# An adaLN block with linear attention and a mixture of experts: new order of the work on every engine, and two f32 products made one split f32r product

## The reference, cut to what matters

```python
mod = (_silu(L0_c) @ L0_wmod).reshape(16, 6, 1, -1)
sa, ca, ga, sb, cb, gb = mod[:, 0], mod[:, 1], ...
ga, gb = sign(g) * max(|g|, 0.25)                      # both gates
h = _layernorm(x) * (1 + ca) + sa
# attention: 16 heads of 8 channels
q, k, v = h @ Wq.T + bq, h @ Wk.T + bk, h @ Wv.T + bv
q = softmax(q over the 8 channels of a head);  k = softmax(k over the tokens)
state = k^T v                                         # 8 x 8 for each head
out = q @ state
out = (out - mu) * rsqrt(var + eps) * ln_g + ln_b
x = x + ga * (out @ Wo.T + bo)
h = _layernorm(x) * (1 + cb) + sb
# experts: the router's softmax over 8, the best 2 of them by probability p
x = x + gb * sum over the two of p_e * (gelu(h @ w_in[e] + b_in[e]) @ w_out[e] + b_out[e])
```

## Time and profile before

| | |
|---|---|
| median of 3 runs | 392.75 us (391.49 to 393.89) |
| profiled execution, its own time | 392.8 us |
| its span (first to last instruction) | 391.1 us |
| TensorE busy | 362.9 us, 93% |
| VectorE busy | 282.5 us, 72% |
| ScalarE busy | 278.5 us, 71% |
| GpSimd busy | 216.8 us, 55% |

### The profile page before, as it was taken

The page is one execution under the profiler, slowest core; times in us unless marked ns, Lnnn a source line. Parts: engine busy times, 40 slices in busy tenths (PEclk is TensorE's granted clock), DMA queues, the critical chain, the costliest instruction groups (busy, mean ns, idle before and its releaser), DMA issues.

```text
span 391.1 us, 8091 instructions
## 1 busy us (share of the span) xinstructions
PE 362.9 (93%) x2502; PEld 327.3 (84%) x2502; DVE 282.5 (72%) x1060; ACT 278.5 (71%) x502; POOL 216.8 (55%) x221
## 2 busy tenths in 40 slices
PE   3657789999999999999999999999999999999995
PEld 3446679889999999899899999898998999988875
DVE  2665586787777888878877778788788787786432
ACT  3333679688787969696887879696969878675740
POOL 2315447373938466483838384664837383754543
PEclk9966579999999999999999999999999999999999
DMA  5570051240706071321606070605224150605061
GB/s 182 151 297 2 0 173 73 80 193 24 247 5 242 29 225 47 157 115 41 231 33 241 3 244 27 240 32 168 106 104 169 38 208 3 217 28 216 32 227 41
DMA packets 18817, 47.83 MB, mean 122 GB/s; under 512 B 2571, under 2 KB 6102, under 8 KB 18518
## 3 DMA queue, kind: packets, MB, share of 16 engines
q1 hardware_dynamic: 18576, 46.90, 33.3%
q10 hardware_dynamic: 198, 0.41, 0.3%
HBM read 42.82 MB, written 4.48 MB: 121 GB/s over the span
## 4 chain that ended last, share of the span: by engine, by line
PE 66%; DVE 9%; issue 6%; DMA 6%; POOL 5%; SPq 4%; ACT 2%; POOLq 0%; DVEq 0%; ACTq 0%
PE pY L684 19%; PE pH L672 6%; PE pH L674 6%; PE pH L673 6%; PE pB L661 4%; PE pQV L641 4%; PE pC L629 4%; PE pC L648 3%; POOL v L355 2%; DVE qn L876 2%; DMA gate_bc<-route_scratch 2%; DMA gates<-gate_scratch 2%; SPq L236 2%; DVE elg_cut L934 2%; PE pA L588 2%
## 5 line engine op out<-in xcount | busy, mean ns | idle before, releaser
L684 PE MATMUL pY<-wout,v 128*128 128x128 f32 x1024 | 128.7, 277 | 1.0 <-DVE v L958 0.7
L684 PEld LDWEIGHTS pY<-wout,v 128*128 128x128 f32 x1024 | 121.7, 193 | 2.2 <-DVE v L958 1.1
L502 ACT ACTIVATE u<-pH,cols 128x512 f32<-128x512 f32 x128 | 86.4, 689 | 49.5 <-PE pH L674 42.8
L344 POOL TENSOR_TENSOR rstd_o<-ve_o,neg_half 128x4 f32<-128x4 f32 x16 | 22.0, 1376 | 104.3 <-DVE ve_o L895 104.3
L958 DVE TENSOR_TENSOR v<-u,gate_bc 128x512 f32<-128x512 f32 x80 | 68.6, 860 | 7.0 <-DMA gate_bc<-route_scratch 3.7
L355 POOL TENSOR_TENSOR v<-u,gate_bc 128x512 f32<-128x512 f32 x48 | 63.7, 1329 | 9.0 <-DMA gate_bc<-route_scratch 9.0
L672 PE MATMUL pH<-h_hi,win_hi 128*128 128x512 f32 x128 | 54.9, 429 | 1.4 <-ACT u L502 1.4
L673 PE MATMUL pH<-h_hi,win_lo 128*128 128x512 f32 x128 | 50.6, 395 | 0.0
L674 PE MATMUL pH<-h_lo,win_hi 128*128 128x512 f32 x128 | 50.5, 394 | 0.0
L349 POOL TENSOR_TENSOR h_lo<-h,h_hi 128x512 fp32r<-128x512 f32 x16 | 22.5, 1405 | 20.2 <-ACT h_hi L440 20.2
L452 ACT ACTIVATE xn<-x_all,nmr,rstd 128x128 f32<-128x128 f32 x64 | 26.2, 482 | 4.5 <-POOL nmr L372 4.5
(11 more groups left out here) (151 smaller groups left out, 781.5 us busy)
## 6 DMA issues: line engine op xcount, KB each, us to landing
gate_bc<-route_scratch SPq DMA_DIRECT2D x64, 512.0 KB, 5.7
x_all<-in_L_attn_x SPq DMA_DIRECT2D x16, 256.0 KB, 6.9
out<-x_all SPq DMA_DIRECT2D x16, 256.0 KB, 2.0
gates<-gate_scratch SPq DMA_DIRECT2D x1, 2048.0 KB, 7.1
gb_bc<-gb_scratch SPq DMA_DIRECT2D x1, 1024.0 KB, 4.6
route_scratch<-gateT SPq DMA_DIRECT2D x64, 4.0 KB
win<-in_L_ffn_w_in SPq DMA_DIRECT2D x1, 512.0 KB, 5.6
wout<-in_L_ffn_w_out SPq DMA_DIRECT2D x1, 512.0 KB, 6.9
```

The costliest lines, as they stand in the source:

```text
L344: pool.tensor_tensor(rstd_o[:, :], ve_o[:, :], neg_half[:, :], ALU.pow).then_inc(s["rstdo_ready"], 1)
L502: act.activation(u[:, e % U, :], pH[:, e % 2, :], ACT.Gelu_apprx_tanh, bias=cols[:, e:e + 1]).then_inc(s["gelu_done"], 1)
L684: i = mm(pY[:, t * P:(t + 1) * P], v[:, e % U, t * P:(t + 1) * P], wout[:, e, :], start=False, stop=(e == NE - 1), skip_group_check=True)
```

## The change

The kernel after computes the same by the same tiles. Nine things differ.

1. `attend_centred` and `attend_project` are one function, `attend`: for each of the four token tiles three f32r products with both halves of the state weights at once (256 columns), q and the state weights each split in a high and a low part. `qT_evac` and `sw_evac` write the high parts, and two new DVE functions, `q_low` and `sw_low`, the low parts. The result goes to `pQV`, where qv of the next batch goes too, so `qv(n)` now waits for `residual1(n - 1)`.
2. Each engine's order is new: the start of it written out call by call, then a loop over a new `step(b)`, on TensorE with the last batches written out too.
3. TensorE runs ahead further: in step `b` the hidden products of `b + 1` stand beside qv and state of `b + 3` and hT and kT of `b + 4`.
4. On ScalarE the exp of the router stands between two gelus; the program has 53 table loads, 33 before.
5. In TensorE's start stand 30 calls of `keep_clock`, an f32 product of 256 columns whose result nobody reads.
6. The gates' and the gain's products come behind hT(0), and `expert_low`, `expert_bias` and the like between the first batches' functions.
7. x of a batch has one of four semaphores, and four loads can be under way.
8. The attention's gates are loaded in two transfers: of the first two batches, and of the others later. `spread_gates` is called once for each of a batch's four parts.
9. Wk and Wo are loaded by ScalarE's queue.

```diff
         def _(sp):
-            sp.dma_start(x_all[:, 0, :, :], x_v[0]).then_inc(s["x_loaded"], DMA)
-            for j, wt in enumerate((Wq, Wv, Wk, Wo)):
+            def load_x(n):
+                w(sp, f"x{n % XS}_loaded", DMA * (n // XS))
+                sp.dma_start(x_all[:, n, :, :], x_v[n]).then_inc(s[f"x{n % XS}_loaded"], DMA)
+
...
+            def spread_first_gates():
                 sp.wait_ge(s["gates_stored"], DMA)
-                sp.dma_start(gates[:, :, :, :].rearrange("p b w c -> p (b w c)"),
-                             gate_scratch.rearrange("(a b) n -> a (b n)", a=1).to_broadcast([P, NB * 2 * P])).then_inc(s["gates_loaded"], DMA)
-
-            def spread_moe_gates():
+                sp.dma_start(gates[:, 0:FIRST, :, :].rearrange("p b w c -> p (b w c)"),
+                             gate_scratch[0:FIRST, :].rearrange("(a b) n -> a (b n)", a=1).to_broadcast([P, FIRST * 2 * P])).then_inc(s["first_gates"], DMA)
+
+            def spread_later_gates():
+                sp.wait_ge(s["gates_stored"], DMA)
+                sp.dma_start(gates[:, FIRST:NB, :, :].rearrange("p b w c -> p (b w c)"),
+                             gate_scratch[FIRST:NB, :].rearrange("(a b) n -> a (b n)", a=1).to_broadcast([P, (NB - FIRST) * 2 * P])).then_inc(s["gates_loaded"], DMA)
+
+            def store_moe_gates():
                 sp.wait_ge(s["gb_ready"], 1)
                 sp.dma_start(gb_scratch, gb_rows[:, :]).then_inc(s["gb_stored"], DMA)
+
...
+                act.activation(qT_hi[:, :], pQT, ACT.Copy).then_inc(s["qT_ready"], 1)
 
             def sw_evac(n):
                 act.wait_ge(s["sw_done"], n + 1)
                 act.wait_ge(s["kinv_ready"], n + 1)
-                w(act, "cen_done", n)
-                w(act, "proj_done", n)
-                act.activation(sw[:, :, :].rearrange("p a c -> p (a c)"), pSW, ACT.Copy, scale=kinv[:, 0:1]).then_inc(s["sw_ready"], 1)
+                w(act, "att_done", n)
...
             def step(b):
+                if has(b + 2):
+                    exp_q(b + 2)
                 if has(b + 1):
-                    ln2_apply(b + 1)
+                    h2_evac(b + 1)
+                if has(b + 3):
+                    h_evac(b + 3)
+                if has(b):
+                    gelu(b, 4)
+                if has(b + 2):
+                    qT_evac(b + 2)
+                    sw_evac(b + 2)
+                if has(b + 1):
+                    exp_router(b + 1)
                 if has(b):
                     gelu(b, 5)
                 if has(b + 2):
-                    exp_k(b + 2)
-                if b == -1:
-                    expert_parts()
-                if has(b + 1):
-                    h2_evac(b + 1)
-                if has(b + 2):
-                    exp_q(b + 2)
-                    ek_evac(b + 2)
-                if has(b + 3):
-                    ln1_apply(b + 3)
-                if has(b + 1):
-                    exp_router(b + 1)
-                if has(b):
-                    gelu(b, 6)
-                if has(b + 2):
-                    sw_evac(b + 2)
-                    qT_evac(b + 2)
+                    out_square(b + 2)
                 if has(b + 1):
                     gateT_evac(b + 1)
                 if has(b):
+                    gelu(b, 6)
...
+            exp_k(0)
+            exp_q(0)
+            ek_evac(0)
+            expert_high()
...
+            def keep_clock():
+                pe.wait_ge(s["siluT_ready"], 1)
+                pe.wait_ge(s["wmod_loaded"], DMA)
+                mm(pH[:, 0, 0:2 * P], ident[:, :], wmod_sb[:, 0:2, :].rearrange("p a c -> p (a c)"), start=True, stop=True)
 
...
-            def attend_centred(n):
-                pe.wait_ge(s["sw_ready"], n + 1)
-                pe.wait_ge(s["qT_ready"], n + 1)
-                for t in range(T):
-                    i = mm(pQT[:, t * P:(t + 1) * P], qT[:, t * P:(t + 1) * P], sw[:, 1, :], start=True, stop=True)
-                i.then_inc(s["cen_done"], 1)
-
-            def attend_project(n):
-                pe.wait_ge(s["sw_ready"], n + 1)
-                pe.wait_ge(s["qT_ready"], n + 1)
-                for t in range(T):
-                    i = mm(pC[:, t * P:(t + 1) * P], qT[:, t * P:(t + 1) * P], sw[:, 0, :], start=True, stop=True)
-                i.then_inc(s["proj_done"], 1)
+            def attend(n):
+                pe.wait_ge(s["swlow_ready"], n + 1)
+                pe.wait_ge(s["qlow_ready"], n + 1)
+                for t in range(T):
+                    o = pQV[:, t, :, :].rearrange("p a c -> p (a c)")
+                    ts = slice(t * P, (t + 1) * P)
+                    mm(o, qT_hi[:, ts], sw_hi[:, :], start=True, stop=False)
+                    mm(o, qT_hi[:, ts], sw_lo[:, :], start=False, stop=False)
+                    i = mm(o, qT_lo[:, ts], sw_hi[:, :], start=False, stop=True)
+                i.then_inc(s["att_done"], 1)
 
...
+                hidden(b + 1, 0)
+                hidden(b + 1, 1)
+                combine(b, 4)
+                hidden(b + 1, 2)
+                hidden(b + 1, 3)
+                combine(b, 5)
+                qv(b + 3)
+                combine(b, 6)
+                combine(b, 7)
+                ek_back(b + 3)
+                hidden(b + 1, 4)
+                h2T(b + 2)
+                hidden(b + 1, 5)
+                hT(b + 4)
+                moe_bias(b + 1)
+                state(b + 3)
+                logits(b + 2)
+                q_turn(b + 3)
+                state_weights(b + 3)
+                combine(b + 1, 0)
+                combine(b + 1, 1)
+                hidden(b + 1, 6)
+                kT(b + 4)
+                attend(b + 3)
+                combine(b + 1, 2)
+                gate_turn(b + 2)
+                hidden(b + 1, 7)
+
+
+            turn_weights()
...
+            def q_low(n):
+                dve.wait_ge(s["qT_ready"], n + 1)
+                w(dve, "att_done", n)
+                dve.tensor_tensor(qT_lo[:, :], pQT, qT_hi[:, :].bitcast(F32), ALU.subtract).then_inc(s["qlow_ready"], 1)
+
+            def sw_low(n):
+                dve.wait_ge(s["sw_ready"], n + 1)
+                w(dve, "att_done", n)
+                dve.scalar_tensor_tensor(out=sw_lo[:, :], in0=pSW, scalar=kinv[:, 0:1], in1=sw_hi[:, :].bitcast(F32),
+                                         op0=ALU.mult, op1=ALU.subtract).then_inc(s["swlow_ready"], 1)
...
-                    state_out(b + 2)
-                    q_norm(b + 2)
-                    k_inv(b + 2)
+                    q_low(b + 2)
+                    sw_low(b + 2)
                 if has(b + 1):
                     gates_out(b + 1)
...
```

More of the change, by code:

```diff
@@ L545, in _ @@
+            exp_k(9)
+            ln2_apply(8)
+            ek_evac(9)
+            for b in range(7, 17):
                 step(b)
@@ new lines, in _ @@
+            kT(2)
+            keep_clock()
+            gate_turn(0)
+            keep_clock()
+            ek_back(2)
+            qv(2)
+            moe_bias(0)
+            hT(3)
+            keep_clock()
+            keep_clock()
+            hidden(0, 0)
+            hidden(0, 1)
+            state(2)
+            kT(3)
+            state_weights(2)
+            hidden(0, 2)
+            q_turn(2)
+            combine(0, 0)
+            hidden(0, 3)
+            hidden(0, 4)
+            h2T(1)
@@ new lines, in _ @@
+            hidden(0, 5)
+            attend(2)
+            hidden(0, 6)
+            combine(0, 1)
+            logits(1)
+            combine(0, 2)
+            hidden(0, 7)
+            qv(3)
+            ek_back(3)
+            combine(0, 3)
+            combine(0, 4)
+            combine(0, 5)
+            state(3)
+            hT(4)
+            hidden(1, 0)
+            gate_turn(1)
+            hidden(1, 1)
+            combine(0, 6)
+            combine(0, 7)
+            state_weights(3)
@@ new lines, in _ @@
+            hidden(1, 2)
+            kT(4)
+            q_turn(3)
+            moe_bias(1)
+            hidden(1, 3)
+            hidden(1, 4)
+            attend(3)
+            hidden(1, 5)
+            h2T(2)
+            combine(1, 0)
+            combine(1, 1)
+            logits(2)
+            hidden(1, 6)
+            combine(1, 2)
+            hidden(1, 7)
+            qv(4)
+            ek_back(4)
+            combine(1, 3)
+            gate_turn(2)
+            combine(1, 4)
+            h2T(3)
```

1098 lines of the change are left out of this document (886 added, 212 removed).

## The result

The changed kernel takes 388.21 us (median of 7 runs, 386.99 to 390.44), the kernel before 392.75 beside it (391.49 to 393.89; also 7 runs, not three): a ratio of 0.989, 95% interval 0.986 to 0.992. That is 4.5 us faster where 17 were forecast, and 1.2 us above the range's upper end. The profiled execution took 388.41 us, with a span of 386.7.

What follows compares the result with a forecast made beforehand. TensorE was taken to bound the kernel: first expert product at 51.5, 313.4 of work behind it, 4.6 idling and 4.5 exit make 374.0 us of span, plus 1.7, about 376 us. The range was 370.5 to 387.

Steps and rivals of the forecast that it cites:

- TensorE's work in a step: Steady step: TensorE's instructions in a row cost 21.05 us before and 20.69 us after the change.
- The order: TensorE's queue: more work stands before the first expert product, leaving 313.4 us behind it, 9.2 less than before.
- Sum: Whole kernel: 51.5 + 313.4 + 4.6 + 4.5 = 374.0 us of span, plus 1.7, about 376 us.
- 2.6 + 1 + 1 = 4.6: TensorE's idling in us: 2.6 at the gate turn over 13 steps, 1 at the end, 1 in early steps.
- 2.3 + 14.6: ScalarE's step: hidden 1 ends 2.3 us in, then 14.6 us without pause; the router's exp was said to end near 17.5.
- The start: Up to the first expert product: h2T(0) near 34.5 to 35.5, gate turn near 45, first expert product at 51.5 us.
- 9.6 us behind it: Start on TensorE: the gate turn keeps its earlier distance of 9.6 us behind h2T(0), so it comes near 45 us.
- saves 0.36: Split product on TensorE: 1.42 us a batch instead of 1.78 for centred plus projection, with VectorE's added work hidden.
- Holes: Rival, chance 0.11: TensorE stays at the lower clock in the start, keep_clocks delay ready work by 13 us; 386 to 390.
- The small first transfer of gates: Start: the first two batches' gates land before the state is ready, worth about 0.5 us.
- two rivals' prices: ScalarE setting the step, 388 us at chance 0.10, and the missing holes in the start, 386 to 390 at 0.11.
- ScalarE sets the step: Rival, chance 0.10: half of ScalarE's waits remain, a step is 21.8 us, 14 us more in all, 388.

Runs made afterwards that it cites:

- e3: Changed kernel with the router's exp replaced by gelu, leaving 35 table loads of 53 (output differs): 391.87 us, ratio 0.996 to the kernel before.
- e1: Changed kernel with the hand-written lists of batches 3 to 7 gone, so the GpSimd, ScalarE and VectorE loops start at 3: 382.68 us.
- e5: Changed kernel with GpSimd's low parts of h and h2 worked out on 128 of 512 columns only (output differs): 382.23 us.
- e10: Changed kernel with both the loops from batch 3 on and GpSimd's low parts of h and h2 on 128 columns (output differs): 382.46 us.
- e9: e1 with expert_bias on VectorE moved behind sw_low(1) and q_low(1): 385.85 us.
- e2: Kernel before with only the split product, in the old order but for the product's own place behind hT: 407.12 us, ratio 1.037 to the kernel before.
- e6: Changed kernel with projection and centred output as two float32 products again, without q_low and sw_low: 390.54 us.
- e11: e1 with projection and centred output as two float32 products again: 386.75 us.
- e4: Changed kernel with all 30 keep_clock products in the start removed: 395.72 us, ratio 1.006 to the kernel before.
- e8: e1 with the gates of all 16 batches in the first transfer instead of two batches first: 386.08 us.
- e7: e1 with state_out ahead of the statistics of the batch five ahead in VectorE's loop: 383.97 us.

## Why the prediction was wrong

- **TensorE's work in a step: right.** A step without waits is 20.58 or 20.59 for the 20.69 counted, the split product 1.42, exit 4.5, and ScalarE is 94% busy there without setting the pace. e3 shows that the added loads do not bound the kernel. A load takes 1283 ns, as the Trainium skill's page "ScalarE: Activation LUTs", section "What ACT_TABLE_LOAD costs", has it; the 2.66 us that it states for a whole switch do not fit: with them ScalarE alone would need 25.2 us a step by the prediction's estimate, and the row of 277.12 has 20.59.
- **The idling, under "The order" and "Sum": wrong, and the main cause of the miss.** The step of the prediction that failed is the term "2.6 + 1 + 1 = 4.6". It took one steady step and used it for all: 0.2 us of waiting in each of 13 steps, all of it at the gate turn, and 1 us for the early steps. Idling and lower clock measured 14.95. Batches 1 to 7 alone lost 10.0; the waits at the gate turn, the only ones with a price, came to 1.6 us behind 60 us. (By the terms of the prediction's own sum, 2.3 + 14.6, the router's exp ends at 16.9, not 17.5, which makes this wait smaller still.) It priced every moved instruction on VectorE at nothing. Those that were moved and held (q_norm, v, the expert bias), all with two SBUF inputs, landed beside GpSimd's operations. The Trainium skill's page "SBUF — State Buffer", section "SBUF: two separate sides", states the exclusion, and the prediction cited it, but asked only whether the *added* operations fall under it. e1, e5 and e10 each win 4.5 to 5.2 us behind the first expert product, and no more together than alone.
- **The start: 2.35 us late.** h2T(0) at 35.8 is a little behind the forecast's 34.5 to 35.5. The gate turn, forecast "9.6 us behind it", came 13.1 behind it: attend(1) waits 2.00 us for q_low, behind the 3.5 us of expert_bias, of which one operation takes 1.39 beside GpSimd's h_lo (0.57 in e5, 0.35 in e9); the first product behind it took 0.55 for 0.36 in e1. The lower clock then made attend(1) 2.69 us long (44.03 to 46.72) where e1 took 1.51. e9 shows that putting the bias later doesn't win the time back.
- **The split product's value, "saves 0.36": right as a price, wrong as a gain in full**: 14 us lost in the old order (e2), 2.3 won in the changed one (e6), 4.1 in e1's (e11).
- **Holes: the rival was rightly held unlikely**; keep_clock is worth 7.5 us (e4). Its "for it" had misread a digit: in the fifth slice of the kernel before TensorE was busy for 0.79, not over 0.8. The small first transfer of gates was undersized: 0.5 for 2.3 in the start and 3.4 in all (e8, in e1's order).
- The range's upper end, 387, stood on two rivals' prices; no case had a start of the loop that differs from its steady state. That case would have been read from the order: written steps on three engines that are not the loop's. The time, 388.2, is close to the 388 of the rival "ScalarE sets the step", but by chance: e3 rules that mechanism out, and its sum ends at 390, since 14 us were added to the span and not to the time. By the chances given, the cases outside the range also add up to about 3 in 10, not 2.

What stays open: about half of the 10.35 us. In e1 the same sum (380.9 - 53.20 - 313.4 - 4.5) still leaves 9.8 us of idling for the 4.6 forecast, with the full clock, and its steps are 21.24 in the mean. e7 shows that the waits for s2T do not account for it; what does was not found. That the exclusion alone explains every long VectorE operation was not tried by itself, and no run took the hold-ups away and left GpSimd's work as it was.

## What to carry to other kernels

Price a new order in every batch that has its own instruction list, not only in the steady one: a loop's step says nothing of the steps ahead of it. For each instruction that a change moves on VectorE or GpSimd, look at what the other of the two runs at that time; an operation on two SBUF inputs can cost 1.75 instead of 0.69 there, and a swap with its neighbour handed the loss on here. Ask also which of the two TensorE waits for: e1 kept a hold-up of v (1.18) for which TensorE did not wait. An instruction saved on one engine by two added on another is worth its price only where the first engine is the limit; measure it in the final order.
